# Fused adaLN block with linear attention and experts: the routing of a group laid under the next group, and 22 more constant products between attention and experts

## The reference

```
h = layernorm(x) * (1 + ca) + sa
x = x + ga * attention_layer(h)       # q, k, v, rotary, elu + 1, two decays per head,
                                      # state M = beta * M + k v^T, y = q M / (q Z + eps),
                                      # layernorm(h + y @ Wo + bo) * gamma + beta
h = layernorm(x) * (1 + cb) + sb
logits = h @ router_w.T               # 8 experts
k_probs, k_idx = top_k(softmax(logits), 2);  k_probs = k_probs / sum(k_probs)
rank = position of the (token, choice) pair among all pairs of its expert, in token order
keep = rank < 641                     # capacity of an expert
out_e = silu(buf_e @ w1_e) @ w2_e     # buf_e: the 641 slots of expert e; 128 -> 512 -> 128
x = x + gb * (sum over 2 choices of k_probs * out[expert, rank] + h)
```

## Time and profile before

| | |
|---|---|
| median of 3 runs | 310.59 us (310.18 to 313.58) |
| profiled execution, its own time | 311.07 us |
| span of the profiled execution | 309.3 us, so 1.8 us lie around it |
| mean granted PE clock | 0.866 of 2.4 GHz |
| PE busy | 257.8 us (83%) |
| DVE busy | 199.4 us (64%) |
| ACT busy | 121.9 us (39%) |
| POOL busy | 88.5 us (29%) |

### The profile page before, as it was taken

How to read it: one execution, slowest core, us unless ns; L and a number is a source line. 1 busy time by engine, 2 the same in 40 slices (tenths; PEclk the granted TensorE clock), 3 DMA queues, 4 the chain that set the end, 5 groups by cost and what they waited for, 6 DMA issues and landing times.

```text
span 309.3 us, 11202 instructions
## 1 busy us (share of the span) xinstructions
PE 257.8 (83%) x4702; PEld 192.0 (62%) x4702; DVE 199.4 (64%) x789; ACT 121.9 (39%) x274; POOL 88.5 (29%) x102
## 2 busy tenths in 40 slices
PE   4995698799889998979887789948999999999900
PEld 2573457586467955668564464424888888888800
DVE  6397879939699396994857468408563344335494
ACT  4377438653375633764312112302243423242300
POOL 0011012200005205252033206630453644455530
PEclk9999759879995599985978695985999999999975
DMA  6999000000000000100001001131224413430456
GB/s 206 282 381 405 28 0 4 5 4 2 3 4 4 21 2 29 31 4 14 12 19 37 13 14 54 43 111 44 73 81 123 156 58 108 137 101 29 158 211 216
DMA packets 18053, 24.97 MB, mean 81 GB/s; under 512 B 2663, under 2 KB 11256, under 8 KB 18002
## 3 DMA queue, kind: packets, MB, share of 16 engines
q1 hardware_dynamic: 14290, 18.97, 18.5%
q0 software_dynamic: 2368, 4.24, 4.2%
q10 hardware_dynamic: 1344, 1.05, 1.0%
HBM read 12.62 MB, written 12.15 MB: 80 GB/s over the span
## 4 chain that ended last, share of the span: by engine, by line
PE 60%; DVE 19%; issue 9%; DMA 5%; ACT 4%; POOL 1%; DVEq 0%; SPq 0%; POOLq 0%; ACTq 0%
PE ps L1849 11%; PE ps L1482 10%; PE ps L1866 8%; PE ps L1589 6%; PE ps L1487 5%; PE ps L1518 4%; PE ps L1631 3%; DVE arena L995 2%; DVE last_p L1404 2%; PE ps L1596 2%; PE ps L1671 2%; PE ps L1686 2%; PE ps L1504 2%; DVE arena L1015 2%; DVE wts L1080 1%
## 5 line engine op out<-in xcount | busy, mean ns | idle before, releaser
L934 ACT ACTIVATE arena<-ps 128x385 f32<-128x385 f32 (+1 forms) x64 | 27.6, 439 | 67.9 <-PE ps L1849 67.2
L674 POOL DMA_INDIRECT pair_out<-arena,meta x40 | 39.2, 980 | 51.1 <-DVE arena L1395 35.0
L620 POOL DMA_INDIRECT dispatched<-row,idx x32 | 31.3, 979 | 65.1 <-PE ps L1596 38.9
L1866 PE MATMUL ps<-w2t,arena 128*128 128x128 f32 x320 | 42.3, 281 | 1.3 <-DVE arena L1395 1.3
L1866 PEld LDWEIGHTS ps<-w2t,arena 128*128 128x128 f32 x320 | 39.9, 191 | 3.5 <-DVE arena L1395 2.7
L1849 PE MATMUL ps<-arena,w1t 128*128 128x256 f32 (+1 forms) x128 | 40.2, 457 | 1.1 <-issue 1.1
L1487 PE MATMUL ps<-later_b,ident_b 128*128 128x512 bf16 x124 | 36.3, 429 | 0.0
L643 POOL TENSOR_TENSOR arena<-arena,ex 128x256 f32<-128x256 f32 x16 | 10.7, 698 | 73.8 <-DVE arena L1015 53.2
L1849 PEld LDWEIGHTS ps<-arena,w1t 128*128 128x128 f32 x128 | 24.2, 200 | 12.0 <-issue 3.8
L1589 PE MATMUL ps<-v,wts 32*32 32x9 f32 x2048 | 23.9, 180 | 8.9 <-issue 7.6
L1589 PEld LDWEIGHTS ps<-v,wts 32*32 32x32 f32 x2048 | 21.9, 116 | 13.9 <-issue 13.6
(11 more groups left out here) (186 smaller groups left out, 437.5 us busy)
## 6 DMA issues: line engine op xcount, KB each, us to landing
dispatched<-fill SPq DMA_DIRECT2D x12, 260.0 KB, 5.1
pair_out<-zero SPq DMA_DIRECT2D x6, 512.0 KB, 6.9
arena<-dispatched SPq DMA_DIRECT2D x8, 325.0 KB, 2.9
w1t<-in_w SPq DMA_DIRECT2D x8, 256.0 KB, 2.6
w2t<-in_w SPq DMA_DIRECT2D x8, 256.0 KB, 2.8
arena<-pair_out SPq DMA_DIRECT2D x4, 512.0 KB, 5.6
const<-in_constants SPq DMA_DIRECT2D x1, 803.0 KB, 6.9
X<-in_x SPq DMA_DIRECT2D x1, 768.0 KB, 8.0
```

The lines of the kernel that those rows point to most:

```text
L620: pool.indirect_dma_start(disp_d, bass.IndirectOffsetOnAxis(ap=idx[:, p.g, t, k:k + 1], axis=0), row[:, p.g, t, k, :], None, bounds_check= ...
L674: pool.indirect_dma_start(pair_d, bass.IndirectOffsetOnAxis(ap=meta[:, u, a, 0:1].bitcast(U32), axis=0), orow[:, u, a, :], None, bounds_ch ...
L934: a_.activation(hid[:, u, f, c0:c0 + cn], ps[:, k % 4, 0:cn], ACT.Silu).then_inc(hid_done[u].sem, 1)
L1866: m = mm(row_bank(u, a)[:, 0:P], hid[:, u, f, 1 + a * P:1 + (a + 1) * P], w2t[:, u, f, :], start=(f == 0), stop=(f == FT - 1))
```

## The change

The routing of a whole group `g - 1` is split. `route` and `choice` stay where they were, at the end of the body. `ranks`, `slot`, `gap`, `weights` and `counted` go into the next body. The rows of `route` go to bank 3 instead of bank 4 where a group `g + 2` follows, so that the other three projections of that group can be made at the end of the body; the wait of a projection on `row_done` is dropped for one ahead of `scores(g, 2)`. The five constant products ahead of `ranks` go for whole groups. `choice` reads the logits from the bank, without the copy. In the half groups `weights` goes ahead of `counted` (first half) and ahead of `slot` (second half). The constant products after the last `ranks` become 52 instead of 34, and 4 stand between the transposes of the first slots and the first up product.

```diff
         def whole(g):
-            return Part(g, g, 0, TG, (T6, T7, T4, T7_top, T4))
+            return Part(g, g, 0, TG, (T6, T7, T4, T7_top, ps[:, 3, :] if g < GROUPS - 2 else T4))
...
             def act_body(g, more):
                 if more:
                     projections(n, 1)
+                if g:
+                    gap(whole(g - 1))
+                if more:
                     values(n)
...
                     pair_rows(whole(g))
-                    gap(whole(g))
...
             def choice(p):
                 dve.wait_ge(lg_ps.sem, lg_ps.now(p.step))
-                v_.tensor_copy(lg[:, at], p.T_l[:, 0:TG * NE].rearrange("p (t e) -> p t e", e=NE)[:, at]).then_inc(lg_done.sem, 1)
-                dve.wait_ge(lg_done.sem, lg_done.now(p.step))
-                apart(dve)
+                lg = p.T_l[:, 0:TG * NE].rearrange("p (t e) -> p t e", e=NE)
...
             def dve_body(g, more):
                 if more:
                     rope_products(n, 0, TG // 2)
+                if g:
+                    slot(whole(g - 1))
                 normed(g, 0)
...
                 normed(g, 1)
+                if g == GROUPS - 1:
+                    weights(whole(g - 1))
+                    counted(whole(g - 1))
                 states(g, 3)
...
                     normed(g, 3)
+                    if g:
+                        weights(whole(g - 1))
+                        counted(whole(g - 1))
                     own_norm(whole(g))
...
                     choice(whole(g))
-                    slot(whole(g))
-                    weights(whole(g))
-                    counted(whole(g))
...
                     second_norm(half_b)
+                    weights(half_a)
                     counted(half_a)
-                    weights(half_a)
                     choice(half_b)
+                    weights(half_b)
                     slot(half_b)
-                    weights(half_b)
...
             def project(g, lo, hi):
-                    elif t and g >= 2:
-                        pe.wait_ge(row_done.sem, row_done.now(g - 2))
...
             def pe_body(g, more):
-                if more:
-                    project(n, 1, TG)
+                if g == GROUPS - 1:
+                    scores(g, 2)
+                    ranks(whole(g - 1))
+                else:
+                    if g:
+                        ranks(whole(g - 1))
+                        pe.wait_ge(row_done.sem, row_done.now(g - 1))
+                    scores(g, 2)
                 adds(g, 2)
-                scores(g, 2)
...
                     route(whole(g))
-                    keep_streaming(ps[:, 0, :], 5)
-                    ranks(whole(g))
+                    if m < GROUPS:
+                        project(m, 1, TG)
...
                     ranks(half_b)
-                    keep_streaming(ps[:, 0, :], 34)
+                    keep_streaming(ps[:, 0, :], 52)
...
-            project(1, 0, 1)
+            project(1, 0, TG)
...
             tr(T6[:, 0:NE], lastx[:, 0:DM]).then_inc(s_lastT, 1)
+            keep_streaming(ps[:, 0, :], 4)
```

More of the change, by code:

```diff
@@ L284, in program @@
         row = sb("row", [P, GROUPS, TG, TOPK, RW])
-        lg = sb("lg", [P, TG, NE])
         mx = sb("mx", [P, TG, NE])
@@ L431, in program @@
         lg_ps = event("logits_ps", 1)
-        lg_done = event("logits_done", 1)
         mx_done = event("top_done", TG)
@@ L437, in program @@
         rk_ps = event("rank_ps", 1)
-        slot_steps = event("slot_steps", 6, "dve")
+        slot_steps = event("slot_steps", 4, "dve")
         idx_done = event("slot_index", 1)
@@ L441, in program @@
         de_done = event("gap_exp", 1)
-        wrow_done = event("row_weights", 2)
+        wrow_done = event("row_weights", 4)
         prow_done = event("row_ids", 1)
@@ L1164, in weights @@
                 dve.wait_ge(de_done.sem, de_done.now(p.step))
-                v_.tensor_scalar(dp[:, at], de[:, at], 1.0, None, ALU.add).then_inc(slot_steps.sem, 1)
-                dve.wait_ge(slot_steps.sem, slot_steps.now(p.step, 5))
+                v_.tensor_scalar(dp[:, at], de[:, at], 1.0, None, ALU.add).then_inc(wrow_done.sem, 1)
+                dve.wait_ge(wrow_done.sem, wrow_done.now(p.step, 1))
                 w_ = row[:, p.g, at, :, DM + 1]
                 v_.reciprocal(w_[:, :, 0], dp[:, at]).then_inc(wrow_done.sem, 1)
-                dve.wait_ge(wrow_done.sem, wrow_done.now(p.step, 1))
+                dve.wait_ge(wrow_done.sem, wrow_done.now(p.step, 2))
                 v_.tensor_tensor(w_[:, :, 1], w_[:, :, 0], de[:, at], ALU.mult).then_inc(wrow_done.sem, 1)
-                v_.scalar_tensor_tensor(shifted[:, at], ef[:, at], float(NE - 1), id_table("to_token", p), ALU.is_equal, ALU.mult).then_inc(slot_steps.sem, 1)
-                dve.wait_ge(slot_steps.sem, slot_steps.now(p.step, 6))
+                v_.scalar_tensor_tensor(shifted[:, at], ef[:, at], float(NE - 1), id_table("to_token", p), ALU.is_equal, ALU.mult).then_inc(wrow_done.sem, 1)
+                dve.wait_ge(wrow_done.sem, wrow_done.now(p.step))
                 v_.tensor_tensor(row[:, p.g, at, :, DM:DM + 1].bitcast(U32).rearrange("p t k o -> p t (k o)"), shifted[:, at],
@@ L1692, in ranks @@
             def ranks(p):
-                pe.wait_ge(lg_done.sem, lg_done.now(p.step))
                 pe.wait_ge(choice_steps.sem, choice_steps.now(p.step, 3))
```

## The result

| | before | after |
|---|---|---|
| median, us | 310.57 (306.41 to 315.63, 20 runs) | 313.22 (310.12 to 315.77, 20 runs) |
| profiled execution, us | 311.07 | 310.12, the fastest of its 20 |
| mean granted PE clock | 0.866 | 0.863 |

The ratio is 1.0121, with a 95% interval of 1.0088 to 1.0155: slower by 1.2% where 1.7% faster was forecast, 305.3 us. The time lies 4 us above the range. In the three later sessions in which this very kernel ran again, all on one chip, it was the faster one (the first measurement does not name its chip). Medians here are of all executions, and ratios leave out those that are over 1.5% above the fastest of their kernel, so a ratio is not the quotient of the medians beside it. There are two things to explain: what the change is worth, and what took it away at the first measurement.

The account below looks back on a forecast made before the run. No engine alone was taken as the bound: PE held 60% of the chain of waits, DVE 19%. Gains of 2.92 + 0.9 + 0.48 + 1.0 = 5.3 us gave 305.8 profiled, 305.3 median; range 302.6 to 309.2.

Parts of the forecast that it names:

- the ranks at the seams: Body seams: ranks ready near 83.6 for slot at 83.93, 0.3 us spare; at the last seam near 165.2, as before.
- PE's unexplained waits falling elsewhere: Anywhere on PE: about 1 us allowed in the range for waits without a visible cause landing in other places.
- Two seams with projections: Bodies 0 to 1 and 1 to 2: rotary products 2.42 us earlier, slot returns 0.96; 1.46 us each, 2.92 together.
- a low stretch lies over a seam: Rival at a new seam: half clock makes projections and ranks late by about 0.8 us each, 306.9 us; chance 0.1.
- Weights and counts: Whole groups: seven instructions, 1.0 us, move behind the body's last normalisation, covered by DVE's 3.92 us wait; worth nothing.
- The last seam: Body 2 to body 3, without projections: normalisation of tile 0 starts near 166.3 against 167.19; 0.9 us gained.
- The last group: Half groups at the end: shorter choice 0.2 us, weights not waiting for counts 0.28; first scatter 0.48 us earlier.
- The sign I named for it: Last group: the half's first scatter was to come less than 1.5 us after POOL's last work.
- Constant products: Before the experts: 52 for 34 keep the clock at 1.00; transposes gain 0.7 us, up products 0.30, 1.0 together.
- the clock falls in the first expert: Rival: about 2.5 us PE gap, then half clock for 6.80 us, costing 3.4, 308.7 us; chance 0.2.
- the rival of the half-clocked stream: Rival before the experts: the 52 constant products run at half clock, 311.5 to 316.2 us; chance 0.04.
- Reading the bank: Maxima and indices read logits from PSUM: taken as nothing, upper bound 0.5 us for a group's eight instructions.

Follow-up runs that it names:

- after_fourth: The changed kernel unaltered, run again in the fourth session: 303.27 us, ratio 0.9874 to the kernel before.
- after_34: The changed kernel with 34 constant products after the last ranks and none before the first up product: 302.08 us, ratio 0.9855 to the kernel before.
- after_fill: The changed kernel with 10 more constant products between the second and third row block of the first expert: 302.11 us, ratio 0.9861 to the kernel before.
- after_third: The changed kernel unaltered, run again in the third session: 301.24 us, ratio 0.9841 to the kernel before.
- routing_back: The kernel before with all of the change except the overlapped routing: 307.92 us, ratio 1.001 to the kernel before.
- after_seam3_back: The changed kernel with PE's order at the last seam as before, five constant products and ranks ahead of the scores: 305.41 us, ratio 0.9976 to before.
- after_again: The changed kernel unaltered, run again in the second session: 302.22 us, ratio 0.9908 to the kernel before.
- after_52_0: The changed kernel with 52 constant products after the last ranks and none before the first up product: 303.01 us, ratio 0.984 to the kernel before.

## Why the prediction was wrong, step by step

**The failed step** is the ranks at the seams: "It fits, with 0.3 to spare" for the two seams with projections, and for the last "The ranks follow near 165.2, about as before". The first takes the last projection and the ranks behind it to run through on PE, the second the short scores of tile 2. In the profile of the first measurement they did not, at the second seam and the third, and DVE waited 1.63 and 5.83 us for ranks. Against the forecast for the profiled execution, 305.8, it took 310.12, 4.3 more; the 7.05 us of waits and the 1.7 of the clock fall are more than that. I put 1 us into the range for "PE's unexplained waits falling elsewhere". What followed shows how large that term is: at like clock the hold-ups cost 6.8 to 7.2 us of the stretch with the first two seams and the wait at the third, and executions of one unchanged kernel had medians of 313.2, 302.2, 301.2 and 303.3 us, while the kernel before moved only between 306.1 and 310.6. The chain's 9% of issue was no warning of it: that is the ordinary wait for instructions, and the later profiles of the changed kernel have 7 to 8% there and took 299 to 304.

**Why it happened at the first measurement** stays open. The order alone is excluded, since three later profiles of this very kernel have the same rows of PE in about 1 us. The 22 constant products and the kernel's own scatters were there too in these three, so neither is enough for it. The low clock alone (T3) is excluded by the profiles of like clock. What is left is the chip or the moment (T5), alone or together with the new order: the kernel before was up by 2.4 to 4.4 us at the first measurement and the changed one by 10 to 12. Late instructions (T1) are excluded for the handfuls, which fit no packet of the instruction queue. That something outside the kernel held PE then is only argued, since no profile shows another's traffic. And the median execution, 3.1 us above the profiled one, has no profile.

**Two seams with projections, 2.92 us.** Right in size where PE runs through. In after_fourth the rotary products of the first seam start 2.05 us after the logits against 4.53 (84.92 less 80.39), 2.48 earlier; slot between them takes 0.87. From the logits to the end of all eight rotary products that is 1.61 us at the first seam and 1.37 at the second, where slot takes 1.15; 1.46 each was forecast. The rival that a low stretch lies over a seam was given 0.1: it came at the third, where half clock made the ranks 1.1 us later in after_34 and after_fill, 0.8 forecast.

**Weights and counts, nothing.** Agrees: DVE's wait for the output product shrank from 3.92 to 3.40 in the same body, and is 1.5 us or more in the later profiles of this kernel.

**The last seam, 0.9.** Without halting, right: mask to `den` is 1.36 us in after_third and 2.44 in routing_back (162.77 to 165.21), both at full clock there, 1.08 less. It is the weights and counts that went from there, as forecast, and not PE's order: after_seam3_back has 1.36 as well. In the first profile it was 6.70.

**The last group, 0.48.** From `rm` of half a to its first scatter it was 3.42 us before (190.67 to 194.09), and 3.14 in after_third (179.75 to 182.89): there the 0.28 came. It is 3.11 in after_fourth, but 3.33 in after_again and the first profile: 0.1 to 0.3 us. No run takes the 0.2 of the shorter choice by itself. The sign I named for it, POOL idle under 1.5 us, was badly chosen: POOL's scatters before it moved too (1.73, 1.72, 1.26 and 0.80 in the four profiles).

**Constant products, 1.0.** From the first transpose of slots to the first up product 2.07 us against 2.63 in the earlier trace rows and in after_34, 0.56 less where 0.7 was forecast; then the first expert takes 12.53 in after_third against 12.80 (210.83 to 223.63), 0.27 less where 0.30 was, since DVE's residuals bound it as forecast. That makes 0.8 us. The rival that the clock falls in the first expert was given 0.2; it came in three of the four profiles of this kernel. Its gap was forecast as 2.5 us and measured 2.57; its stretch was 3.4 us and not 6.80, so it costs 1.65 us and not 3.4. Where it comes it takes back the 0.8 and as much again. The reason I gave against the rival of the half-clocked stream, that constant products precede each rise, was also a wrong reading of the trace: of the eight low stretches of the kernel before that end in a rise, the last ends among up products, and those of bodies 1 and 2 (at 106.9 and 147.9) behind transposes and output products.

**Reading the bank, nothing.** Right. The median MAX8 takes 156 ns from the bank and 152 from SBUF, FIND_INDEX8 165 and 160: 0.04 us for a group. The rule of the Trainium skill (VectorE: DVE Perf Modes, The TRN2 errata) would have made it about 0.5 us by my estimate from its cycles; these rows do not agree with it. The upper bound had no need to be 0.5 either: another scaling of 128 columns from a bank, L987 of the kernel before, takes 286 ns, as little as the one from SBUF. But the removed copy is worth next to nothing at the first seam either, for ACT ends last there.

**The sum.** 5.3 us of 310.6 is a ratio of 0.983. The later sessions gave 0.9908, 0.9841 and 0.9874 for the very kernel, 2.8, 4.9 and 3.9 us (by the medians of all executions 3.9, 5.6 and 4.6). So the sum is somewhat too large, by the fall in the first expert for one thing, and the forecast failed by the one term that no row of the kernel before could size. That the later sessions lie near it does not make the first forecast right.

## What to carry to other kernels

When work that another engine waits for is put behind a run of many short products, the wait inherits the hold-ups of that run: 5.83 us at one seam in one execution, 0.41 in the others at full clock. Price that into the range before the change is made. Idle time that the profile calls issue need not stay unexplained: set its ends against the packets of the instruction queue. Putting the few products that release somebody ahead of the many is no proven cure: the hold-up at the second seam took in ranks that stood ahead, and the kernel with the old order at the last seam was no faster. A gain of 1 to 2% on one core should be measured in more than one session before it is believed, or given up: here the same pair gave 1.012 and 0.984. Compare two profiles only at like granted clock, stretch by stretch; 20 us more at half clock made some 5 us here. Removing an instruction pays only where its engine ends last, so read what released the next one.

## What the runs showed of the hardware

- PE waits for its own instructions, by these traces: 134 of its 142 stops that follow no semaphore wait end 1.2 to 1.55 us after a 16 KB packet of the instruction queue. These stops cost 4 to 11 us in a profile without added traffic and 16 to 17 with 40 us at a DMA share near 1.00, where single ones last up to 4.2 us.
- PE can also stop inside independent 32-row products in a way that fits no such packet: in one profile (after) in six handfuls over 6.4 us, at a DMA share of 0.17.
- Full DMA engines for 40 us cost this kernel 9 to 11 us, though no engine waited for these transfers.
- The same gap of 2.56 us on PE was followed by 3.4 us at half clock in nine profiles (the first, after_again and after_fourth among them) and by full clock in two (after_third, after_52_0).
- One unchanged kernel had 10 to 31 us at half clock in the same stretch of its work in different executions, and took 75.1 to 78.0 us for it at 10 to 24 us.
